# First attention: one head in four of the spread keys moved from VectorE to ScalarE

## The reference, cut to what matters

```
xh  = layernorm(h).reshape(b, n, 12, 16)
qkv = einsum('bnhd,hde->bnhe', xh, W_qkv) + b_qkv
q, k, v = split(qkv, 3)
scores = einsum('bihd,bjhd->bhij', q, k) / sqrt(192)
h = h + (softmax(scores) @ v).reshape(b, n, 192) @ W_out + b_out
```

## Time and profile before

| | |
|---|---|
| median of 3 runs (lowest, highest) | 1230.18 us (1229.3, 1230.34) |
| the profiled execution's own time | 1230.62 us |
| its span, first to last instruction | 1228.8 us |
| busy: PE, ACT, DVE, POOL | 1152.7, 868.4, 934.2, 457.6 us |
| TensorE's mean granted clock | 0.982 of full speed |
| busy in 206 to 241 us: idle of VectorE before L784 | 3.8 us of 35 |
| an undisturbed pass, turn_qk(g+1, 1) to the next one | 229.36 to 236.97, 7.6 us |
| first and last spread_k (L845), 22 of them | starts at 93.1 and 279.8 us |

### The profile page before, as it was taken

How to read it: one execution, slowest core, us unless ns; L and a number is a source line. 1 busy time by engine, 2 the same in 40 slices (tenths; PEclk the granted TensorE clock), 3 DMA queues, 4 the chain that set the end, 5 groups by cost and what they waited for, 6 DMA issues and landing times.

```text
span 1228.8 us, 26757 instructions
## 1 busy us (share of the span) xinstructions
PE 1152.7 (94%) x8874; PEld 1000.6 (81%) x8874; DVE 934.2 (76%) x2392; ACT 868.4 (71%) x3173; POOL 457.6 (37%) x479
## 2 busy tenths in 40 slices
PE   6998788988899999999999999999988998999998
PEld 3996666667788888888888888888876777799998
DVE  5668898896899999999877787788763789555433
ACT  2676778977788888888888888888873643544432
POOL 0001031023333443344333444443461500999854
PEclk9999989999899999999999999999998999999999
DMA  9402002000000000000030000000004543555200
GB/s 373 158 1 79 1 2 78 2 1 2 2 2 2 2 2 1 2 1 1 2 82 2 2 2 2 1 2 1 2 23 165 187 180 109 165 162 176 83 9 16
DMA packets 30357, 64.04 MB, mean 52 GB/s; under 512 B 4623, under 2 KB 26879, under 8 KB 28927
## 3 DMA queue, kind: packets, MB, share of 16 engines
q1 hardware_dynamic: 30220, 62.32, 15.4%
HBM read 43.73 MB, written 18.58 MB: 51 GB/s over the span
## 4 chain that ended last, share of the span: by engine, by line
PE 64%; DVE 17%; ACT 14%; issue 4%; DMA 0%; POOL 0%; SPq 0%; DVEq 0%; POOLq 0%; ACTq 0%
ACT t_p L1283 7%; PE bank L1609 6%; PE bank L381 5%; DVE f_eq L2070 4%; PE bank L1583 4%; PE bank L1531 4%; PE bank L1600 3%; PE bank L1574 3%; PE bank L1551 3%; PE bank L1535 3%; PE bank L1532 3%; PE bank L1533 3%; PE bank L1534 3%; PE bank L2179 2%; PE bank L2175 2%
## 5 line engine op out<-in xcount | busy, mean ns | idle before, releaser
L1283 ACT ACTIVATE t_p<-bank,t_nmax 108x108 f32<-108x108 f32 x792 | 270.3, 368 | 36.4 <-DVE t_nmax L784 35.5
L1111 POOL TENSOR_TENSOR t_sq<-t_raw 108x768 f32<-108x768 f32 x88 | 154.5, 1756 | 134.4 <-ACT t_raw L1231 133.5
L2304 POOL TENSOR_TENSOR f_hid_lo<-f_hid,f_hid_hi 128x432 fp32r<-128x432 f32 (+2 forms) x144 | 143.0, 1018 | 98.5 <-ACT f_hid_hi L2290 97.9
L1283 ACT ACTIVATION_READ_ACCUMULATOR t_p<-bank,t_nmax 108x1 f32 x792 | 177.1, 224 | 0.0
L801 DVE TENSOR_TENSOR t_p<-t_p,t_rinv 108x432 f32<-108x432 f32 x198 | 152.0, 768 | 6.8
L784 DVE TENSOR_REDUCE t_nmax<-bank 108x2 f32<-108x216 f32 (+1 forms) x242 | 121.8, 518 | 42.8 <-PE bank L1574 24.1
L2290 ACT CAST f_hid_hi<-f_hid 128x432 fp32r<-128x432 f32 (+2 forms) x144 | 73.1, 515 | 100.0 <-DVE f_hid L2261 56.7
L1583 PE MATMUL bank<-ident,t_p 108*108 108x108 f32 x792 | 109.4, 261 | 23.7 <-ACT t_pT L1291 21.5
L1583 PEld LDWEIGHTS bank<-ident,t_p 108*108 108x108 f32 x792 | 80.9, 132 | 56.8 <-ACT t_pT L1291 34.8
L1291 ACT COPY t_pT<-bank 108x432 f32<-108x432 f32 x198 | 107.0, 541 | 25.6 <-PE bank L1583 25.6
L1119 POOL TENSOR_TENSOR t_xl<-t_xt,t_xh 128x108 fp32r<-128x108 f32 x44 | 18.8, 427 | 235.6 <-DVE t_xh L752 235.6
(11 more groups left out here) (229 smaller groups left out, 3316.2 us busy)
## 6 DMA issues: line engine op xcount, KB each, us to landing
spilled<-f_slot SPq DMA_DIRECT2D x76, 216.0 KB, 1.9
f_slot<-spilled SPq DMA_DIRECT2D x76, 216.0 KB, 2.7
A_x<-in_x SPq DMA_DIRECT2D x5, 1728.0 KB, 18.5
A_w<-in_tok_w SPq DMA_DIRECT2D x5, 768.0 KB, 7.1
f_raw_down<-in_w_proj SPq DMA_DIRECT2D x1, 2304.0 KB, 11.2
out_tokens<-h SPq DMA_DIRECT2D x21, 81.0 KB
f_raw<-in_w_mfc SPq DMA_DIRECT2D x3, 512.0 KB, 4.7
f_raw<-in_w_mfc SPq DMA_DIRECT2D x6, 256.0 KB, 6.4
```

Source lines behind the costliest of these rows:

```text
L1111: pool.tensor_tensor(sq, v, v, ALU.mult).then_inc(s["sq"], 1)
L1283: act.activation(b.p[g % 2][:, m, :], self.scores_of(g, m), ACT.Exp, bias=b.nmax[:, m:m + 1], accum_out=b.rsum[:, m:m + 1]).then_inc(s["ex ...
L2304: pool.tensor_tensor(self.hid_lo[m % 4][:, c], self.hid[m % 4][:, c], self.hid_hi[m % 4][:, c].bitcast(F32), ALU.subtract).then_inc(s["lo" ...
```

## The change

VectorE's `spread_k` writes only the heads j = 0, 1, 2 of each tile (128 x 972 elements). A new `spread_fourth` on ScalarE writes head 3 of each tile (128 x 324) from the same bank as Identity with a scale and a bias from `row_of`, which gets a fifth column of zeros for the bias. It waits for `spread_k` of the same group (`kev`) and counts a new semaphore `k4`, for which `turn_qk(g, 1)` and every `scores(g, c)` wait besides.

```diff
-    row_of = fixed("row_of", [128, 4])
+    row_of = fixed("row_of", [128, 5])
...
-            shape = [128, 3, 4, GT]
-            dve.tensor_tensor(b.kS[g % 2][:, :, :].rearrange("p (t j) n -> p t j n", j=4),
+            shape = [128, 3, 3, GT]
+            dve.tensor_tensor(b.kS[g % 2][:, :, :].rearrange("p (t j) n -> p t j n", j=4)[:, :, 0:3, :],
                               src.unsqueeze(2).to_broadcast(shape),
-                              self.row_of[:, :].unsqueeze(1).unsqueeze(3).to_broadcast(shape),
+                              self.row_of[:, 0:3].unsqueeze(1).unsqueeze(3).to_broadcast(shape),
                               ALU.mult).then_inc(s["kev"], 1)
...
+        def spread_fourth(g):
+            self.evacuated(act, "qk", g, 0)
+            after(act, s["S"], self.scored(g - 2))
+            src = self.turn_bank("qk", g, 0)[:, 0:3 * GT].rearrange("p (a n) -> p a n", a=3)
+            to = b.kS[g % 2][:, :, :].rearrange("p (t j) n -> p t j n", j=4)[:, :, 3, :]
+            act.activation(to, src, ACT.Identity, scale=self.row_of[:, 3:4], bias=self.row_of[:, 4:5])\
+               .then_inc(s["k4"], 1)
...
+            spread_fourth(0)
             copy_qk(0, 1)
             yield
...
             next_begins(g, 0)
+            if g + 1 < GROUPS:
+                spread_fourth(g + 1)
             if this:
                 exps(g, 1)
...
             if kind == "B":
+                if u == 1:
+                    pe.wait_ge(s["k4"], g + 1)
                 self.evacuated(pe, "x", g)
...
             if kind == "B":
+                pe.wait_ge(s["k4"], g + 1)
                 after(pe, s["exp"], nth(g, 12, 4 * c - 1) - 4)
```

More of the change, by code:

```diff
@@ L629, in __init__ @@
         names = ("stats mv log rstd xf xd T Tev xh xl Q Qev sq ss norm qn S max exp rinv rg pn PV PVev "
-                 "O h hb kev gate_d gate_a init").split()
-        absent = "xd xh xl sq ss norm qn rg hb gate_d gate_a".split() if small else ()
+                 "O h hb kev k4 gate_d gate_a init").split()
+        absent = "xd xh xl sq ss norm qn rg hb gate_d gate_a".split() if small else ["k4"]
         self.s = {n: sem(f"{kind}_{n}") for n in names if n not in absent}
@@ L2445, in layouts @@
     A["image_of"] = np.repeat(np.eye(GROUP_IMAGES, dtype=f), TOKENS, 0)
-    A["row_of"] = np.repeat(np.eye(4, dtype=f), 32, 0)
+    A["row_of"] = np.pad(np.repeat(np.eye(4, dtype=f), 32, 0), ((0, 0), (0, 1)))
     A["owner"] = full_depth(np.repeat(np.eye(GROUP_IMAGES, dtype=f), TOKENS, 1))
```

## The result

The changed kernel takes 1231.6 us, the median of 22 executions (1228.3 to 1604.29); the kernel before 1228.37 us (22 executions, 1224.21 to 1230.34). The ratio is 1.0033, with a 95% interval from 1.0023 to 1.0043: **slower by 0.33%**, clear of the 0.2% that can be told from no change. The forecast time, 1231.8 us, was hit almost to the digit, but partly by luck: it stood on a median of 3 runs, 1230.18 us, which 22 runs put 1.8 us lower. What counts is the difference: +1.6 us forecast, +3.2 us measured between the medians and +4.1 between the means, which the ratio compares; by its interval, 0.23 to 0.43%, it is 2.8 to 5.3 us. The forecast difference is too small by 1.2 us at least.

The account below looks back on a forecast made before the run. TensorE's pieces (output, turn_qk, scores) were taken to bound undisturbed passes, with VectorE having slack. Terms 0.9 + 0.2 + 0 + 0.5 = +1.6 us on a 1230.18 us median gave 1231.8 us, range 1229.1 to 1234.3.

Parts of the forecast that it names:

- End of the tokenizer, +0.9: turn_qk(0, 1) waits for spread_fourth(0), delaying second_moment(21) and finish(21), so TensorE enters the attention 0.9 us later.
- Passes 0 and 1, +0.2: row_max(0, 2) starts 1.42 us later, spread_k(2) gives back 0.34; +1.1 us for the whole start, 0.2 of it here.
- Pass 20, +0.5: spread_fourth(21) goes ahead of exps(20, 1) where ScalarE has no gap, moving it and scores(21, 0): +0.5 us.
- Undisturbed passes 0: Steady passes, 206 to 241 us: spread_fourth fits ScalarE's 0.53 us gap before exps(g, 1), so 0 us.
- waits 0: TensorE's four `k4` waits a pass cost nothing where fulfilled; upper bound 1.8 us, taken as 0.
- (a): VectorE's saving arrives in the passes: all 22 give -7.4 us, 1222.8 us, half of them 1226.5; chance 9%.
- (b): ScalarE becomes the bound: some 20 passes each keep 0.17 us, +3.4 us on top of the ends, 1235.2 us; chance 8%.
- The lower clock, 0: The sum holds no term for TensorE's stretches at the lower clock, 1.2 instead of 2.4 GHz.
- The likeliest case: The prediction's own forecast, 1231.8 us, own range 1231.0 to 1232.6; chance 50%.
- rival (c): A shift of 1 us may add one more TensorE stretch at the lower clock, 1.7 us: 1233.5 us; chance 18%.
- within 0.2%: Outcome for the whole kernel: indistinguishable from no change, neither below 1227.7 nor above 1232.6 us; chance 60%.
- slower: Outcome for the whole kernel: above 1232.6 us; chance 31%.

Follow-up runs that it names:

- 3: Changed kernel with ScalarE taking its head only in groups 2 to 20, VectorE all heads in groups 0, 1 and 21; 1228.29 us, ratio 0.9998.
- 7: As 6, with second_moment(21) ahead of turn_qk(0, 1) on TensorE and root(21) ahead of copy_qk(0, 1) on ScalarE; 1229.03 us, ratio 1.0015.
- 5: Changed kernel with ScalarE spreading fourth heads only in groups 2 to 21, VectorE all of groups 0 and 1; 1228.13 us, ratio 1.0017.
- experiment 1: The changed kernel run again with nothing edited; 1231.84 us, ratio 1.0026 to the kernel before.
- 11: As 9, plus 6 idle products ahead of turn_p(g-1, 1) in passes 3 to 10, 16 and 17; 1228.77 us, ratio 0.9998.
- 12: As 10, plus 6 idle products ahead of turn_p(g-1, 1) in passes 3 to 10, 16 and 17; 1227.57 us, ratio 0.9992.
- 2: Kernel before with only the four `k4` waits a pass added on TensorE, always already fulfilled; 1229.33 us, ratio 0.9997.
- 10: Kernel before with 10 idle products on TensorE ahead of scores(0, 0); 1228.97 us, ratio 1.0006.
- 4: Changed kernel with VectorE still writing all four heads and ScalarE writing the fourth again; 1234.86 us, ratio 1.0048.
- 6: Changed kernel with ScalarE spreading fourth heads only in groups 0 to 20, VectorE all of group 21; 1229.67 us, ratio 1.0018.
- 8: Changed kernel with idle TensorE products, 16 ahead of turn_qk(0, 1) and 12 ahead of scores(0, 0); 1233.51 us, ratio 1.0052.
- 9: Changed kernel with idle TensorE products, 8 ahead of turn_qk(0, 1) and 5 ahead of scores(0, 0); 1231.74 us, ratio 1.0029.

## Why the prediction was right, and where it wasn't

- **End of the tokenizer, +0.9.** Right: +0.94, by turn_qk(0, 1) behind ScalarE's head, and second_moment(21) behind it. Undoing both ends (3) gives the time back; mending the order alone (7) moves finish(21) as the reasoning says, but not the time, since copy_qk(0, 1) is late next. The prediction looked at one follower of turn_qk(0, 1) and not at the other; that did not change the sum.
- **Passes 0 and 1, +0.2.** Right: with the clock held, the start costs 1.14 us up to spread_k(4), so this term is 0.2. row_max(0, 2) got the wait that was named. The saving that makes up for it came one and two passes later than forecast: nothing in step 1 to 2, which is 0.53 us longer, then 0.2 and 0.15.
- **Pass 20, +0.5.** Right at its place, +0.50 at exps(20, 1); behind it the scores of group 21 are 0.65 later, so the term is 0.15 short. Alone (5) this end costs 0.17% (0.03 to 0.32%).
- **Undisturbed passes 0, waits 0.** Right: 7.60 to 7.61 us in every trace, 0.9997 for the waits. Rivals (a) and (b) fell. The Trainium skill's rule of rival (b), "ScalarE: Activation LUTs", "Rules for kernel authors", which sends multiplications to VectorE, holds here in engine time (0.67 us on ScalarE for 0.34 saved) but not in the time of a pass, where the gap hid it.
- **The lower clock, 0.** This is the step that failed. The likeliest case took no change in the stretches at the lower clock, and gave one more of them, rival (c), +1.7 us, 18%. The bare terms came out as 1.14 + 0.65 = 1.8 us, forecast 1.6. Measured are 3.2 us between the medians and 4.1 between the means (2.8 to 5.3), so 1 us at least, and 1.1 (means of experiment 1) to 2.3 us (means of the result) as an estimate, lies outside the terms of the sum: an amount like one stretch more of rival (c). It lifts the outcome from "within 0.2%" (60%) to "slower" (31%). That it is the clock is likely, not proved. For it: with the waits filled the cost is 1.15 us, where the result has 4.1, and in the traces of 11 and 12 no fall is left between the first and the last spread_k. Against it: the three rows above. The traces are too few to settle it; between those two places the clock falls 3, 4, 4 and 2 times in before, 2, 3 and 10, and 3, 3, 6, 3, 4, 5 and 3 times in 1, 4, 5, 6, 7, 8 and 9. The Trainium skill, "TensorE: Matmul & The Clock Gate", "What's actually happening", that the throttled clock is the default and activity releases it, agrees: unread products in the waits took the mean clock from 0.9824 and 0.9837 to 0.9895.
- **The base and the range.** The 1231.8 us lay on the measured time because two misses cancel, a base 1.8 us too high and a difference 1.6 us too small between the medians. And the range, 1229.1 to 1234.3, leaves 1.0 us below rival (c)'s 1230.1 and 0.8 above its 1233.5, not the half that the text names.

What stays open is where. The start alone was filled in 9 without a gain in the median, so the extra falls are not all there; and a fall in one execution is absent in the next. One place can be pointed at: between 243 and 262 us the traces of 1, 5, 6, 7, 8 and 9 have a fall or two, and of the others only 2 and 10 have one. That the change shifts TensorE's waits against whatever decides a fall was only argued. Open too is the 0.6 us between the 1.8 of the traces and the 1.15 between the means of 11 and 12; the intervals of these ratios, 0.1% or 1.2 us to each side, are wider than that. No version beats the kernel before beyond its interval; 12 comes nearest, at 0.9992 (0.9981 to 1.0003).

## What to carry to other kernels

Work moved off an engine that is waited for by nobody buys next to nothing (here 0.35 of 7.4 us), however well it fits into a gap of the receiving engine; look first at the ends of the pipeline, where the order isn't the steady one and a moved instruction stands behind things that it never stood behind before. Follow every later instruction on the waiting engine, and after mending one, ask which is late next. Give a change of TensorE's clock a term of its own in the sum: here what the waits leave unexplained, 1.1 to 2.3 us, was about as large as all the new waits together. A single trace gave the clock's change with the wrong sign, and the mean clock of many executions gave its size only as an estimate; the firmest sign was to fill the waits in both kernels and compare them.

## What was not expected of the hardware

- The same wait is followed by a fall in one pass and not in the next. In the trace of before TensorE waits 1.66 us ahead of one turn_p(g-1, 1) and 1.67 us ahead of the next, and only the second is followed by an output at the lower clock:

```profile
124.68 0.58 PE L1583 MATMUL bank<-ident,t_p 108*108 108x108 f32 x4 [1.66 <-ACT t_pT L1291]
125.09 1.14 PE L1609 MATMUL bank<-oB,t_oT 128*108 128x192 f32 x6
...
133.90 0.58 PE L1583 MATMUL bank<-ident,t_p 108*108 108x108 f32 x4 [1.67 <-ACT t_pT L1291]
134.32 2.06 PE L1609 MATMUL bank<-oB,t_oT 128*108 128x192 f32 x6
```

- Among executions of the changed kernel the time follows the mean granted clock: 0.976 went with 1236 to 1237 us and 0.986 with 1228.3 and 1229.1 us. Among those of the kernel before it doesn't: at 0.986 alone the spans in the batch of experiment 1 go from 1223.5 to 1228.4 us.
